# Eight store addresses per register load on SyncE, and the carry's column computed ahead of TensorE's wait, in a graph network with a count matrix

## The reference

```python
# network 0, three layers, batch norm and relu between them
h = einsum('ni,rio->nro', x, weight)          # 8 tables of messages, one per edge type
msg = h[src, etype]
agg = segment_sum(msg * norm[:, None], dst)   # norm: 1 / edges of that (dst, type)
x = agg + x @ root + bias
# network 1: three hops of a normalised neighbour sum
msgs = cur[col] * edge_weight[:, None]
cur = segment_sum(msgs, row)
```

## Time and profile before

| | |
|---|---|
| median of 3 runs | 5420.99 us (5415.71 to 5423.11) |
| span of the profiled execution | 5488.9 us |
| instructions | 69373 |
| passes 0, 1, 2 in the profile, first to last visit's matmul | 380 to 1578, 1735 to 3046, 3159 to 4478 us |
| TensorE, VectorE, ScalarE, GpSimd busy | 71%, 59%, 20%, 49% |

### The profile page before, as it was taken

One profiled execution on the slowest core, in us unless ns is written; L12 is line 12 of the kernel. 1 busy time (PEld: TensorE's weight loads), 2 busy tenths in 40 slices (PEclk: granted clock), 3 DMA queues, 4 the chain that ended last, 5 costly groups with the idle time before them and its releaser, 6 DMA issues.

```text
span 5488.9 us, 69373 instructions
## 1 busy us (share of the span) xinstructions
PE 3923.0 (71%) x14159; PEld 1986.1 (36%) x14160; DVE 3234.1 (59%) x8826; ACT 1109.9 (20%) x1906; POOL 2705.8 (49%) x2646
## 2 busy tenths in 40 slices
PE   7026766777767776777766866766676668999997
PEld 3013333333333333333333333333333334444443
DVE  7955455444435666666666466666666666546364
ACT  4000000000013333333333433333333340000000
POOL 0666677666643666666666066666666630000000
PEclk9556666656568898989999989898999989999998
DMA  6011111111124333333433534333343337888895
GB/s 228 3 38 45 47 45 46 45 46 46 46 101 161 118 117 117 119 118 119 119 115 115 216 105 119 117 119 115 118 120 115 118 92 267 295 295 300 292 301 166
DMA packets 416183, 716.67 MB, mean 131 GB/s; under 512 B 98515, under 2 KB 322056, under 8 KB 415535
## 3 DMA queue, kind: packets, MB, share of 16 engines
q1 hardware_dynamic: 331562, 544.93, 29.2%
q0 software_dynamic: 84096, 166.09, 12.4%
q10 hardware_dynamic: 130, 1.20, 0.1%
HBM read 431.85 MB, written 279.93 MB: 130 GB/s over the span
## 4 chain that ended last, share of the span: by engine, by line
PE 42%; issue 21%; SPq 9%; POOL 8%; DVE 7%; another core or an unknown queue 5%; DMA 4%; ACT 3%; DVEq 0%; ACTq 0%; POOLq 0%
PE psum L928 13%; PE psum L976 7%; PE psum L977 7%; PE psum L915 6%; POOL area L597 6%; SPq L475 4%; SPq L476 4%; PE psum L905 4%; PE psum L876 3%; POOL key_list L567 3%; ACT bufE L647 2%; DMA area<-msg_table,visit_src 2%; DMA counts<-bufE 1%; DVE agg_and L1637 1%
## 5 line engine op out<-in xcount | busy, mean ns | idle before, releaser
L597 POOL DMA_INDIRECT area<-msg_table,visit_src x2490 | 2524.8, 1014 | 1562.3 <-issue 595.7
L928 PE MATMUL psum<-area 128*128 128x256 f32 x4980 | 1883.9, 480 | 365.9 <-DMA area<-msg_table,visit_src 121.4
L1637 DVE TENSOR_TENSOR agg_and<-agg_and,psum 128x256 f32 x1245 | 523.0, 420 | 1351.0 <-PE psum L928 660.0
L928 PEld LDWEIGHTS psum<-area 128*128 128x128 f32 x4980 | 1025.4, 234 | 805.6 <-issue 552.2
L647 ACT CAST bufE<-psum 128x512 f16<-128x512 f32 x1507 | 883.4, 586 | 1784.4 <-PE psum L915 718.3
L915 PE MATMUL psum<-bufE,carry 128*128 128x512 f16 x1506 | 641.5, 426 | 799.7 <-issue 466.2
L1607 DVE TENSOR_SCALAR area<-iota,agg_and 128x256 f32<-128x256 f32 x2490 | 884.5, 417 | 16.7 <-ACT agg_and L663 12.6
L976 PE MATMUL psum<-area,edge_area 128*128 128x512 f16 (+1 forms) x1911 | 688.9, 368 | 15.5 <-DVE edge_area L1663 9.5
L915 PEld LDWEIGHTS psum<-bufE,carry 128*128 x1506 | 147.8, 98 | 1525.1 <-issue 1519.7
L977 PE MATMUL psum<-area,edge_area 128*128 128x512 f16 (+1 forms) x1911 | 688.2, 368 | 0.0
L905 PE MATMUL psum<-bufE 128*128 128x512 f16 x1507 | 622.9, 413 | 0.7 <-issue 0.7
(11 more groups left out here) (326 smaller groups left out, 1891.8 us busy)
## 6 DMA issues: line engine op xcount, KB each, us to landing
area<-counts SPq DMA_DIRECT2D x252, 896.0 KB, 4.5
counts<-bufE SPq DMA_DIRECT2D x1507, 128.0 KB
msg_table<-area SPq DMA_DIRECT2D x147, 512.0 KB, 2.6
area<-msg_table,visit_src POOLq DMA_INDIRECT x2490
agg_and<-counts SPq DMA_DIRECT2D x162, 128.0 KB, 4.5
area<-counts SPq DMA_DIRECT2D x21, 224.0 KB, 3.1
bufE<-inv_sqrt SPq DMA_DIRECT2D x2, 1568.0 KB, 11.6
out<-cur SPq DMA_DIRECT2D x12, 256.0 KB
```

The source lines that it names most:

```text
L597: g.indirect_dma_start(out=msg[:, n % MV, :], out_offset=None, in_=msg_table, in_offset=bass.IndirectOffsetOnAxis(ap=visit_src[:, v:v + 1] ...
L928: t.matmul(psum[:, banks[c % len(banks)], at:at + W2], msg[:, n % MV, :], visit_sel[:, n % SV, :], start=v % 2 == 0, stop=v % 2 == 1).then ...
L1637: v.tensor_tensor(to, to, psum[:, banks[c % len(banks)], at:at + W2], ALU.add).then_inc(visit_added, 1)
```

## The change

SyncE: `store_blocks` loads eight addresses (or fewer, at the start and the end of a pass) with one call, ahead of the wait, keeps them in registers, and gives no bounds for them. TensorE: `count_block` calls `compute_val` on `column * 2`, the byte offset of the column, ahead of the wait for `block_kept`.

```diff
+STORES = 8
...
-                for m in range(blocks_built(k), blocks_built(k + 1)):
+                last = blocks_built(k + 1)
+                for m in range(blocks_built(k), last):
+                    if m % STORES == 0 or m == blocks_built(k):
+                        upto = min(m - m % STORES + STORES, last)
+                        addresses = nc.values_load_multi_w_load_instructions(
+                            store_at[0:1, m:upto], engines=(mybir.EngineType.SP,))[1]
+                        begin = m
+                    at = addresses[m - begin]
                     sp.wait_ge(block_kept, m + 1)
-                    at = sp.value_load(store_at[0:1, m:m + 1], min_val=0, max_val=(NSLOT - 1) * BW)
                     sp.dma_start(counts_dram[:, bass.ds(at, BW)], kept[:, m % KR, :]).then_inc(block_stored[m % KR], 16)
...
                         column = ((carry[0] << by) if by >= 0 else (carry[0] >> -by)) & 128
+                        pe.compute_val(column * 2)
                         pe.wait_ge(block_kept, m)
                         last = t.matmul(psum[:, 4 + m % 3, :], carry16[:, bass.ds(column, 128)], kept[:, (m - 1) % KR, :], start=False, stop=True)
```

## The result

| | before | changed |
|---|---|---|
| median of the timed runs | 5418.35 us (5400.49 to 5423.11, 4 runs) | 5363.93 us (5356.81 to 5368.55, 4 runs) |
| span of the profiled execution | 5488.9 us | 5354.7 us |
| passes 1 and 2, first to last visit's matmul | 1311, 1319 us | 1251, 1260 us |

The ratio is 0.9898, 95% interval 0.988 to 0.9915: 1.0% faster, 54 us. The forecast was 5055, the range ended at 5270. The measured time lies above it.

The account below looks back on a forecast made before the run. SyncE's store queue was taken to bound both passes, 1.71 us a store. Passes of 1123 us (floor 1060 plus 63) would save 378 of 2624 us, taken as 365: 5421 to 5056, forecast 5055 us, range 4960 to 5270.

Parts of the forecast that it names:

- the floor of 1060 us a pass: Passes 1 and 2: GpSimd's gathers at 1.26 us a visit need 1046 us, plus some 15 us for last chunks.
- the excess of 504 us: Passes 1 and 2: their 2624 us less two floors, 2120 us; claimed as all the change can win.
- SyncE's service: SyncE's time per store: 1.71 us, 1.07 work and 0.64 stall, forecast to fall to 1.11 us, 0.78 plus 0.33.
- The load of 1.427 us in the hops: SyncE in the hops: one slow load beside an undisturbed median, read as stalls coming mainly where instructions are dense.
- (a): SyncE's stores: stalls stay with the DMA, service 1.42 us, total 5110 us; chance 0.17.
- (d): SyncE's load of eight holds the ring of buffers, 5.7 us a load, slower at 5510 us; chance 0.04.
- (e): SyncE's queue: the same stalls fill whatever time is freed, nothing changes, 5421 us; chance 0.04.
- TensorE's part: Cast-to-carry chain: three register operations move ahead of the wait, 1.33 to 1.05 us a block; no gain term of its own.
- (b): TensorE's carry matmul doesn't take the precomputed value, chain stays 1.33 us, 5115 us, as the first part alone; chance 0.13.
- TensorE's catching up: After a stall, the shorter chain lets TensorE regain 0.34 us a block instead of 0.06.
- a quarter: Each pass's 252 us excess: half the stall time gone, half the rest's harm covered, so 63 us stays.
- (c): Passes without stores exceed the floor too: pass 0 takes 1198 us, so passes end at 1200, total 5200 us; chance 0.12.

Follow-up runs that it names:

- the parts alone: Only SyncE's loads of eight, then only TensorE's precomputed column, each added to the kernel before (5473.11 us): 5416.10 us, ratio 0.9885, and 5470.83 us, 0.9998.
- the second check: One more address load with its bounds check per store: on the kernel before (4913.52 us) 5266.79 us, ratio 1.072; on the changed kernel 4914.09 us, 0.9996.
- the loads alone: Changed kernel without compute_val, so only SyncE's loads of eight, against the kernel before: ratio 0.9885 beside 5473.11 us, 1.0003 beside 4909.13 us.
- the column alone: Kernel before plus only TensorE's compute_val of the column, against the kernel before: ratio 0.9998 beside 5473.11 us, 0.999 beside 4909.13 us.

## Why the prediction was wrong

The step that failed is the floor of 1060 us a pass, with the excess of 504 us over it that SyncE was to give back. The mechanism on SyncE was right, but a second bound stood close below it.

**The bound.** SyncE's queue bounded both passes, as read from its waits, and only there is a gain: shown by the parts alone on a disturbed occasion (1.15% and 0.02%); the second check (7.2% against 0) shows that work in this queue can bound a pass.

**SyncE's service.** FUSED_REGOPS and SEQ_ASSERT went, as said. The load of eight was priced at its upper bound of 2.14 us; it takes 0.528, so each register after the first costs (0.528 - 0.267) / 7 = 0.037 us. The Trainium skill's 200 ns for each register in bulk ("Runtime: NRT & Kernel Launch", section "Instruction fetch mechanics") doesn't hold for this load; the page speaks of loads from HBM, and these addresses lie in SBUF. Clean work is then 0.51 + 0.07 = 0.58 us a store where I said 0.78. The stalls fell further than to half: of SyncE's register operations other than loads, 705 of 6030 lasted over 0.5 us before, 45 of 3016 after. (The load of 1.427 us in the hops was no sign of them: undisturbed, the longest of that line takes 1.512.) So this term erred to the cautious side, and rivals (a), (d) and (e) fall, though the measured time lies nearer to the 5421 of (e) than to the forecast: SyncE's queue did empty, and the time hardly followed.

**TensorE's part.** I took 0.28 us off the chain; the undisturbed casts are 1.131 us apart in place of 1.332, so 0.20. The address takes the precomputed value, but one operation stays behind the wait; line 923 has one ALU_OP left (compare). Changed kernel, undisturbed:
```profile
L923 PEldq ALU_OP  x1506: 36/36/36, 1587.8 to 3901.3; - x189
```
Rival (b) falls by this. Its remark that the first part alone would do as much is right all the same, though not its time of 5115: the second part gave nothing measurable, since undisturbed the gathers cover the chain, and TensorE's catching up, on which I counted, didn't show on the disturbed occasion either.

**The sum, where it failed.** "The excess over it is 2624 - 2120 = 504 us, and that is all the change can win", and of that only "a quarter" stays. The floor of 1060 was right for an undisturbed occasion (1046 and 1053 without blocks). But on the disturbed occasions, and only there, the counts of TensorE come late too, and with them the visits themselves, whatever SyncE does; that both have one cause is likely, since both are absent without gathers, but not shown. The trace had it: pass 0, without one block, took 1198 us. Rival (c) named that row, with a chance of 0.12, and I argued it away with the planning on VectorE; undisturbed, with the same planning, pass 0 takes 1075. If the visits of passes 1 and 2 are held as those of pass 0 are, which no run shows apart, the 504 us divide so: 2 x 123 are the visits' own holds; 2 x 41 are what a pass of 1101 has above 1060 when undisturbed; and 2 x 60 is what the change won in the trace. Some 56 us are left for late counts in the chain of blocks. Where I wrote that half of the stall time would be gone and half of the rest be covered, a pass kept 195 of its 252 us.

**Reading a wait.** ScalarE's 173.3 us on unplaced semaphores I put down to stores. They were TensorE's late counts: all 52 of those casts start within 0.06 us of a recorded count of `block_carried`, and so do all 84 of the 259.3 us after the change. Only the 152.8 us were stores, and these did go. The stores that SyncE brought late cost less than half of what I took them for.

**The base.** The span of the profiled execution before was 68 us above the median of its runs and above all four of them, near the 5471 to 5473 of the later disturbed occasions; the changed kernel's own is within 10 us of its runs. The two traces are thus not a fair pair: their passes differ by 119 us, the timed runs by 54, and later by 57 (the loads alone) and 71 (the change). The traces of one occasion agree with the timed runs: from the column alone, which takes the time of the kernel before, to the loads alone the passes shrink by 26 and 27 us. So of the 2 x 60 us above some 53 to 71 are the change's gain; the others belong to the base, and a pass kept more of its excess than the 195 us. For the whole difference of base I took 13 us off.

## What to carry to other kernels

When register operations that usually take 0.02 to 0.15 us last 0.7 us in one queue, don't count that as this queue's own work that a leaner queue would save: look at a stage where the queue is idle, and see whether that stage too is longer than its work. Give a wait without a releaser to no one until the semaphore's own update is found. A leaner queue pays only while that queue is the bound, and only down to the next bound: here adding work to the queue showed that it can bound a pass, and taking it away showed how close the next bound lay. And measure the kernel before again beside every experiment: here it moved by 11%, some ten times the gain.

## What the runs showed of the hardware that was not expected

- The same kernel takes 4909 to 4922 us or 5418 to 5473 us, 11% apart, depending on the occasion; the difference lies in the three passes (1075, 1100, 1101 against 1198, 1311, 1319 us), with 26 us more between passes 0 and 1, not behind them (1009 against 1011 us from the last visit to the end).
- On the slower occasions some of SyncE's register operations take 0.7 us, a few 1.4, and TensorE's matmuls are counted up to several us late and then 0.035 us apart; the trace also lacks a quarter and more of the updates' records. In the one run without GpSimd's 2474 gathers no register operation is stalled, no count comes more than 0.8 us late, and the records are all but complete.
- A load of eight registers from SBUF takes 0.528 us, of one 0.267.
- Register loads whose value nobody uses, and which have no bounds, are dropped before they reach the chip; with bounds they stay, and one of them with its check lengthened a store from 1.07 to 1.70 us.
